# A sparse-attention block in which VectorE's step is turned round and the pass that pushes scores down goes to GpSimd

## What is computed

```python
x = x + layernorm(attn(layernorm(x)))
x = x + layernorm(ffn(layernorm(x)))

# attn
k = concat([mem_k, x @ Wk]); v = concat([mem_v, x @ Wv])
dots = einsum('bhid,bhjd->bhij', q, k) * 64 ** -0.5
dots = einsum('bhij,hk->bkij', dots, pre_proj)
dots = where(jj - 16 > ii, -max, dots)              # causal, memory keys are seen by all
vk = top_k(dots, 64)[0][..., -1:]                   # the 64th largest of each row
dots = where(dots < vk, -max, dots)
attn = einsum('bhij,hk->bkij', softmax(dots), post_proj)
out = (attn @ v) @ Wo + bo

# ffn
down((silu(gate(x)) * up(x)))                       # weights int32 / 127
```

## Time and profile before

| | |
|---|---|
| median of 3 runs | 3637.55 us (3636.05 to 3637.64) |
| the profiled execution, time | 3636.07 us |
| the profiled execution, span from first to last instruction | 3634.3 us |
| busy VectorE / ScalarE / TensorE / GpSimd | 3292.4 / 3199.3 / 2795.9 / 1551.4 us |
| mean granted TensorE clock | 0.884 |

### The profile page before, as it was taken

One profiled execution on the slowest core, in us unless ns is written; L12 is line 12 of the kernel. 1 busy time (PEld: TensorE's weight loads), 2 busy tenths in 40 slices (PEclk: granted clock), 3 DMA queues, 4 the chain that ended last, 5 costly groups with the idle time before them and its releaser, 6 DMA issues. The chain is left out here.

```text
span 3634.3 us, 67348 instructions
## 1 busy us (share of the span) xinstructions
PE 2795.9 (77%) x13751; PEld 1808.7 (50%) x13751; DVE 3292.4 (91%) x12492; ACT 3199.3 (88%) x9018; POOL 1551.4 (43%) x2663
## 2 busy tenths in 40 slices
PE   7777778777777878778778867877777788877765
PEld 3455455545545545555455545544555455545544
DVE  4699999999999999999999999999999999999994
ACT  1799999999979999999999979998999999999973
POOL 3233444444434444444444444443444444444433
PEclk9888999988888899888998888899889998899886
DMA  1000000000000000000000000000000000000000
GB/s 41 7 2 2 5 8 5 8 2 5 8 4 8 5 8 2 5 8 5 8 5 7 2 4 8 5 8 2 5 8 5 8 5 8 2 5 8 2 7 4
DMA packets 31375, 22.37 MB, mean 6 GB/s; under 512 B 3201, under 2 KB 30338, under 8 KB 30722
## 3 DMA queue, kind: packets, MB, share of 16 engines
q1 hardware_dynamic: 30722, 16.03, 1.6%
HBM read 11.83 MB, written 4.19 MB: 4 GB/s over the span
## 5 line engine op out<-in xcount | busy, mean ns | idle before, releaser
L871 ACT ACTIVATE signs<-scores,state 128x528 int8<-128x528 f32 (+3 forms) x3072 | 1764.3, 574 | 181.8 <-DVE state L1149 103.4
L713 PE MATMUL s_bank<-xn,gT 128*128 128x512 f32 (+3 forms) x2048 | 900.6, 568 | 1.7 <-issue 0.7
L1269 POOL TENSOR_SCALAR probs<-probs,rinv 128x528 f32<-128x528 f32 (+3 forms) x1024 | 547.1, 553 | 507.3 <-DVE rinv L1053 507.3
L737 PE MATMUL t_bank<-ident,probs 128*128 128x128 f32 x2560 | 482.7, 313 | 299.1 <-POOL probs L1269 289.7
L724 PEld LDWEIGHTS y_bank<-u_all,probsT 128*128 128x128 f32 x5120 | 619.9, 194 | 133.4 <-issue 124.2
L724 PE MATMUL y_bank<-u_all,probsT 128*128 128x128 f32 x5120 | 625.2, 278 | 7.1 <-ACT probsT L882 7.1
L1260 POOL TENSOR_TENSOR offset<-consts,found 128x36 f32<-128x36 f32 x256 | 161.7, 632 | 1047.5 <-DVE work L1014 1047.5
L871 ACT ACTIVATION_READ_ACCUMULATOR signs<-scores,state 128x1 f32 x3072 | 575.7, 187 | 0.0
L737 PEld LDWEIGHTS t_bank<-ident,probs 128*128 128x128 f32 x2560 | 299.7, 153 | 506.8 <-issue 398.6
L1048 DVE SCALAR_TENSOR_TENSOR probs<-scores,kth,expo 128x528 f32<-128x528 f32 (+3 forms) x1024 | 522.8, 565 | 24.8 <-issue 19.1
L892 ACT ACTIVATE expo<-scores,negmax 128x528 f32<-128x528 f32 (+3 forms) x1024 | 535.0, 575 | 0.0
(11 more groups left out here) (148 smaller groups left out, 3384.9 us busy)
## 6 DMA issues: line engine op xcount, KB each, us to landing
xwork<-in_L_attn_x_dram SPq DMA_DIRECT2D x17, 256.0 KB, 2.8
xres<-in_L_attn_x_dram SPq DMA_DIRECT2D x16, 256.0 KB, 2.9
out_dram<-ybuf SPq DMA_DIRECT2D x16, 256.0 KB, 2.4
u_all<-in_L_attn_Wq_dram SPq DMA_DIRECT2D x1, 512.0 KB, 3.7
u_all<-in_L_attn_Wk_dram SPq DMA_DIRECT2D x1, 512.0 KB, 4.5
u_all<-in_L_attn_Wv_dram SPq DMA_DIRECT2D x1, 512.0 KB, 5.3
u_all<-in_L_attn_Wo_dram SPq DMA_DIRECT2D x1, 512.0 KB
expo<-in_L_ffn_w_gate_dram SPq DMA_DIRECT2D x1, 192.0 KB, 4.7
```

The source lines that it names most:

```text
L713: nc.tensor.matmul(score_part(t, 0, KEYS[t]), lhsT=gT[s % 2][:, t * P:(t + 1) * P], rhs=xn[par][:, 0:KEYS[t]], start=True, stop=False, ski ...
L737: mm = nc.tensor.transpose(t_bank[q % 2][:, at:at + P], probs[:, h % 2, KEY_AT[t] + j * P:KEY_AT[t] + (j + 1) * P], ident[:, :])
L871: nc.scalar.activation(signs[:, k, 0:ROW[t]], row(scores, ring(head_of(s, k + 1), RING), t), ACT.Sign, bias=guesses(s % STATES, k, GUESSES ...
L1269: nc.gpsimd.tensor_scalar(prb, prb, rinv[:, slot_p, t:t + 1], 1.0, ALU.mult, ALU.mult).then_inc(scaled, 1)
```

## The change

- The push-down leaves VectorE. GpSimd does it in four instructions, one a tile, `work = scores - work`, once the count of that tile is there; a new semaphore `hidden` counts them. It subtracts 1 and not FMAX, so all scores are kept scaled by 2^-60 (the factor goes into `a_all`, `amem`, the guess table, `minus_unit` and the exponential's `scale`), and the causal mask is -2^40.
- VectorE's step is turned round. It begins with the four MAX8, pick and kth of head g-5 (the head that was counted one step earlier), with the flag loaded between the second and the third MAX8; then two counts of head g-4, the masked products and `rinv`, the other two counts, the eviction, `spread` and `missed`, the LayerNorm statistics, memory maxima or feed-forward product of that step, and the guess chain at the end.
- GpSimd's step: `negmax`, seed, memory scores, scaling, then the four push-downs, `offset`, `pmem`.
- TensorE makes the third part of the transposes ahead of the flag's matmul, ScalarE takes it ahead of the flag.
- Of the extras of a batch, U 8 to U 15 and DOWN move to other places of the list, the feed-forward product on VectorE from s = 10 to 12 to s = 11 to 13, the last LayerNorm from s = 14 to s = 15.

```diff
-MASKED = -2.0 ** 100
+UNIT = 2.0 ** -60
+MASKED = -2.0 ** 40
...
-                        turn(head_of(s, LAG_P), g - LAG_P, 0)
-                        turn(head_of(s, LAG_P), g - LAG_P, 1)
+                        for q in range(3):
+                            turn(head_of(s, LAG_P), g - LAG_P, q)
-                    if lagged(kind, s, LAG_P):
-                        turn(head_of(s, LAG_P), g - LAG_P, 2)
...
+                                                 scale=1.0 / UNIT
...
+                    if applies:
+                        dve.wait_ge(hidden, 4 * gp + 4)
+                        alone(dve)
+                        for p, t in enumerate(ORDER):
+                            if p == 2:
+                                dve.wait_ge(misc_free, flag_index(kind, b, s) + 1)
+                                alone(dve)
+                                rows_missed = dve.value_load(flags[0:1, T:T + 1].bitcast(I32), min_val=0,
+                                                             max_val=2 ** 31 - 1)
+                            v.max(candidates(past)[:, t, 1:9], work[:, AT[t]:AT[t] + ROW[t]]).then_inc(select_step, 1)
+                        dve.wait_ge(offset_ready, gp + 1)
+                        dve.wait_ge(select_step, T + 1)
+                        v.scalar_tensor_tensor(out=offset[:, :, 0:9], in0=offset[:, :, 0:9], scalar=0.0,
+                                               in1=candidates(past), op0=ALU.is_equal,
+                                               op1=ALU.mult).then_inc(select_step, 1)
+                        dve.wait_ge(select_step, T + 2)
+                        dve.sem_clear(select_step)
+                        v.tensor_reduce(kth[:, bass.ds(slot_p, 1), :].squeeze(1), offset[:, :, :], AX_X,
+                                        ALU.add).then_inc(kth_ready, 1)
                     if selects:
                         guessed = guesses(now, GUESSES, 1)
                         dve.wait_ge(guess_ready, g - 1)
                         dve.wait_ge(mem_placed, gk + 1)
                         dve.wait_ge(masked, 4 * gk + 4)
                         alone(dve)
-                        count_found(ORDER[0])
-                        count_found(ORDER[1])
+                        for t in ORDER[:2]:
+                            count_found(t)
                     if applies:
-                        dve.wait_ge(misc_free, flag_index(kind, b, s) + 1)
-                        alone(dve)
-                        rows_missed = dve.value_load(flags[0:1, T:T + 1].bitcast(I32), min_val=0, max_val=2 ** 31 - 1)
-                    if selects:
-                        count_found(ORDER[2])
-                        count_found(ORDER[3])
...
+                    if selects:
+                        for t in ORDER[2:]:
+                            count_found(t)
...
+                    if selects:
+                        dve.wait_ge(found_ready, 4 * gk + 4)
+                        v.scalar_tensor_tensor(out=spread[:, :], in0=found[:, :], scalar=-2.0 * AIM, in1=found[:, :],
+                                               op0=ALU.add, op1=ALU.mult).then_inc(select_step, 1)
+                        dve.wait_ge(select_step, 1)
+                        v.scalar_tensor_tensor(out=missed[:, 0:T], in0=spread[:, :], scalar=WINDOW ** 2 + 0.5 - AIM ** 2,
+                                               in1=active, op0=ALU.is_gt, op1=ALU.mult,
+                                               accum_out=missed[:, T:T + 1]).then_inc(bad_ready, 1)
...
+                    if 11 <= s < 11 + HC and kind != "first":
+                        c = s - 11
+                        dve.wait_ge(silu_pool, HC * (b - 1) + c + 1)
+                        v.scalar_tensor_tensor(out=f_up[:, c, :], in0=f_tanh[:, c, :], scalar=1.0,
+                                               in1=f_up[:, c, :], op0=ALU.add, op1=ALU.mult).then_inc(silu_ready, 1)
...
-                        v.scalar_tensor_tensor(out=work[:, :], in0=work[:, :], scalar=-FMAX,
-                                               in1=scores[:, bass.ds(slot_k, 1), :].squeeze(1),
-                                               op0=ALU.mult, op1=ALU.add).then_inc(select_step, 1)
...
-                    def top_scan():
-                        if selects:
-                            dve.wait_ge(select_step, 2)
-                            for t in ORDER:
-                                v.max(candidates(now)[:, t, 1:9], work[:, AT[t]:AT[t] + ROW[t]]).then_inc(select_step, 1)
...
-                    if lagged(kind, s, LAG_K):
-                        at_least(pool, kth_ready, g - LAG_K)
-                        pool.wait_ge(found_ready, 4 * (g - LAG_K) + 4)
...
+                    if lagged(kind, s, LAG_K):
+                        gk, slot_k = g - LAG_K, ring(head_of(s, LAG_K), RING)
+                        for p, t in enumerate(ORDER):
+                            pool.wait_ge(found_ready, 4 * gk + p + 1)
+                            alone(pool)
+                            wrk = work[:, AT[t]:AT[t] + ROW[t]]
+                            nc.gpsimd.tensor_tensor(wrk, row(scores, slot_k, t), wrk, ALU.subtract).then_inc(hidden, 1)
+                        at_least(pool, kth_ready, gk)
+                        alone(pool)
+                        nc.gpsimd.tensor_tensor(offset[:, :, 0:9], ranks, found[:, :].unsqueeze(2).to_broadcast([P, T, 9]),
+                                                ALU.add).then_inc(offset_ready, 1)
+                    if lagged(kind, s, LAG_P):
...
```

More of the change, by code:

```diff
@@ L84 @@
           11: [("GATE", 2), ("UP", 2)],
[L85 to L88, removed]
+          12: [("U", 10), ("U", 11)],
+          13: [("U", 12), ("U", 13)],
+          14: [("DOWN", 0), ("DOWN", 1)],
+          15: [("U", 14), ("U", 15)]}
 AIM = TOPK - 4
@@ L418, in build @@
         found_ready = sem("found_ready")
+        hidden = sem("hidden")
         offset_ready = sem("offset_ready")
@@ L913, in step @@
                     exponentials(3)
+                    take_turned(2)
                     if flagged(kind, s):
@@ L1063, in step @@
                                             accum_out=rowmax[:, bass.ds(slot, 1), t]).then_inc(masked, 1)
+                    if selects:
[6 more added lines that the diff above has]
+                                               accum_out=missed[:, T:T + 1]).then_inc(bad_ready, 1)
+                    if s == 0 and kind in ("first", "mid"):
+                        dve.wait_ge(x_in, 16 * (b + 2))
+                        norm_stats(kind, b, "x", xwork)
+                    if s == 8 and kind in ("first", "mid"):
+                        memory_maxima(kind, b, 1 - par)
                     if s == 6 and kind != "first":
@@ L1071, in step @@
                         norm_stats(kind, b, "X1", xres)
-                    if s == 14 and kind != "first":
+                    if 11 <= s < 11 + HC and kind != "first":
[3 more added lines that the diff above has]
+                                               in1=f_up[:, c, :], op0=ALU.add, op1=ALU.mult).then_inc(silu_ready, 1)
+                    if s == 15 and kind != "first":
@@ L1286, in step @@
                                               head_mem(smem[par], s)).then_inc(mem_placed, 1)
+                    gp, slot_p = g - LAG_P, head_of(s, LAG_P) % 2
+                    if lagged(kind, s, LAG_P):
+                        pool.wait_ge(rinv_ready, gp + 1)
+                        at_least(pool, probs_ready, 4 * gp + 4)
+                        alone(pool)
+                        for t in SCORE_ORDER:
+                            prb = probs[:, slot_p, AT[t]:AT[t] + ROW[t]]
+                            nc.gpsimd.tensor_scalar(prb, prb, rinv[:, slot_p, t:t + 1], 1.0, ALU.mult,
+                                                    ALU.mult).then_inc(scaled, 1)
+                    if lagged(kind, s, LAG_K):
[6 more added lines that the diff above has]
+                        at_least(pool, kth_ready, gk)
+                        alone(pool)
+                        nc.gpsimd.tensor_tensor(offset[:, :, 0:9], ranks, found[:, :].unsqueeze(2).to_broadcast([P, T, 9]),
+                                                ALU.add).then_inc(offset_ready, 1)
+                    if lagged(kind, s, LAG_P):
+                        if s == LAG_P and kind != "first":
+                            pool.wait_ge(misc_full, misc_index(kind, b, ("PM", 1)) + 1)
+                        pool.wait_ge(scaled, 4 * gp + 4)
+                        alone(pool)
+                        nc.gpsimd.tensor_copy(head_mem(pmem, head_of(s, LAG_P)), mem_parts(probs[:, slot_p, :])).then_inc(pmem_ready, 1)
                     extras(kind, b, s)
```

86 lines of the change are left out of this document (17 added, 69 removed).

## The result

| | before | after |
|---|---|---|
| median, us | 3637.6 (3636.05 to 3639.61, 4 runs) | 3796.25 (3793.69 to 3801.88, 4 runs) |
| ratio, 95% interval | | 1.0438 (1.042 to 1.0456) |
| span of the profiled execution, us | 3634.3 | 3800.0 |

The change makes the kernel 4.4% slower. The forecast was 2.4% slower (3724 us). The direction and the mechanism held; the size was off by 72 us. The time lies at the very end of the range of 3550 to 3800, and 6 us above the narrower 3660 to 3790 that the forecast had for itself.

A forecast was written before the change was run, and what follows sets the result against it. VectorE (201.3) and ScalarE (199.1 of 213.3 us a batch) bound it nearly level; 2.3 us of waiting replace 1.8 removed a plain step. 5.85 us times 14.5 batches is 85, plus 6, minus 3: 3636 + 88 = 3724 us, range 3550 to 3800.

The forecast's parts named there:

- L1124 and L1128 pass, L1131 loses to the fourth: VectorE's guess chain after L1123: two links get in at a pass boundary, the next stands until GpSimd's fourth pass ends, 11.8.
- the tail: End of the last batch before the change, where the guess chain meets back-to-back GpSimd passes and VectorE gets in at boundaries.
- the link that I had at 1.12 us from the end: L1139 in VectorE's guess chain: from it to the next MAX8 1.12 us, undisturbed after the fourth pass.
- Steps with extras: Steps with LayerNorm statistics 13.95 us each, memory maxima 13.85, s = 10 14.1, s = 11 and 12 14.6, s = 13 13.7.
- the sum: All steps of a batch added up: 219.15 us against 213.3, so 5.85 us a batch more.
- The upper end of the range: 3800 us, for GpSimd passes of 4.0 us in all: 0.4 to 0.5 us a step, 88 + 75 above.
- The reordering … I price at nothing: Turned step order, flag load between MAX8s, scaled constants and moved extras: the same instructions on the same engines, no cost.
- `missed` slips in: Rival, 0.18: `missed` gets in with `spread` at a pass boundary, plain steps 12.85, about 212 us a batch, 3616 us.
- The removed instruction was not the limit: Rival, 0.09: ScalarE is at its end in plain steps and the gain elsewhere is eaten, no change, 3637 us.
- ScalarE becomes the bound: Rival, 0.15 with waiting halved (3458 to 3560): ScalarE's stream limits at about 201.6 us a batch, 3458 us.
- GpSimd keeps the memory through its four passes: Rival, 0.10 with slower passes: `spread` stands until 11.8, plain step 14.0, batch near 235, about 3965 us.

The follow-up runs named there:

- e1: The changed kernel with its turned order kept but the push-down back on VectorE as one instruction between `spread` and `missed`: 3564.38 us, ratio to before 0.9794.
- e2: The changed kernel with GpSimd's four passes reading and writing `work` alone (times -1, scores left out, so results differ from the reference): 3497.66 us.
- e3: The changed kernel with GpSimd's four passes only writing `work` (memset, no read, push-down left out, so results differ from the reference): 3464.89 us.
- e10: The changed kernel with GpSimd's four push-downs merged into one instruction of 1344 columns behind the scaling: 3866.19 us.
- e9: The changed kernel with one wait, for all four counts, ahead of GpSimd's four push-downs and none between them: 3793.42 us.
- e7: e5 with the flag's load and two of the counts ahead of the products, and the one-input extras ahead of MAX8: 3852.62 us, ratio 1.0592.
- e5: The changed kernel with VectorE's order changed so that scaling and push-down on GpSimd meet only single-input counts, eviction and MAX8: 3767.79 us, ratio 1.0355.
- e11: e1 with only the flag's register load moved, from between the second and third MAX8 to right ahead of the branch: 3677.42 us.

## Why the prediction was right, and where its size was off

**Direction and mechanism: right.** The four passes take 1.30, 1.03, 0.77 and 0.57 us in the mean (forecast 1.30, 1.03, 0.75, 0.48; the fourth takes 0.49 in all but three steps of a batch), stand right behind the scaling, and lie over `spread`, `missed` and the guess chain. `spread` and `missed` were to end at 9.65 and 10.65 us of the step; they end at 9.56 and 10.55. `pmem` fell from 1.45 to 0.24 us, and MAX8 waits for `hidden` for 4 us in the whole run. ScalarE's idle time ahead of its counts grew by 0.86 us a step, where half a microsecond was forecast. e1, e2, e3 and e10 show the cause by taking it away, weakening it and making it longer.

**The step that failed is "L1124 and L1128 pass, L1131 loses to the fourth".** (In the changed kernel L1123, L1124, L1128 and L1131 are L1128, L1129, L1133 and L1136.) I took from the tail that a second instruction can follow on one that got in. In the changed kernel one passes at each boundary and no more. L1129 loses to the fourth pass too, 0.54 us, and the chain goes on from L1133 at 1715.74 instead of from the link that I had at 1.12 us from the end: 1.67 us are left. Against that the passes end at 11.70 of the step and not at 11.8. The plain step is 13.30 to 13.33 and not 13.05, 1.9 us a batch in seven steps. e9 rules out that GpSimd's waits make the difference to the tail; why L1124 and L1128 both got in behind L1123 there is open. The tail's passes have one input, but with one-input passes in e2 `missed` and L1129 stand as well (`missed` 461 and L1129 318 ns).

**Steps with extras: too low by about as much again.** From `rinv` to `rinv`, the 14 middle batches grew by 135.4 us, 9.67 each, where the sum had 5.85. Of these 3.8 us, 1.9 are those of the plain steps, and 0.25, 0.8 and 0.2 come from s = 10, 11 and 12 (14.35, 15.4 and 14.8 us in the mean against 14.1, 14.6 and 14.6). The rest, some 0.7, is spread over the others: s = 13 has 0.3 of it, and s = 1, 2 and 4, which the sum took for plain, are at 13.6, 13.8 and 13.5 in the mean. In s = 11 to 13 the sum had the feed-forward product at its 0.61 us and named it a two-input instruction, but gave neither it nor GpSimd a wait for it: the product takes 1.33 us there instead of 0.69, and GpSimd's fourth pass, which meets it, 0.9 instead of 0.49. 14 x 3.8 = 53 us of the missing 72 are in the middle batches. The first batch grew by 14.8 and not 6 us, and the last one by 12.2: I had spared both without ground, as every step in them has the same collision.

**The upper end of the range was reached in another way than the one that it was made for.** It stood for passes of 4.0 us in all, and they took 3.5. Its sum doesn't come out either: 0.4 to 0.5 us a step over some 240 steps is 96 to 120 us, not 75. That the time lies inside by 4 us is luck in part.

**"The reordering … I price at nothing" was wrong too, and hid in the sum.** e1 shows that the turned order, with the moved extras, gains 73 us: without the searches its batches take about 208.4 us against 213.2, its plain steps 12.0 to 12.9, 12.5 in the mean as before. The gain comes in steps with extras, where the guess chain's links that stood for GpSimd's work in the old order (by the names of before product L1128 363 ns, L1149 287, L1123 238 in the mean) are at 183, 197 and 165 in e1. One of these collisions has only moved: in s = 10 to 12 it is `missed` that now stands for `f_up * f_gate` (338 ns in the mean, 186 before). Which part of the change gives the gain was not tried apart. So the move of the pass costs 6.5% of e1, and the reordering hides a third of it.

**The rivals.** "`missed` slips in" falls with 955 ns. "The removed instruction was not the limit" (3637 us) falls with 159 us of change. "ScalarE becomes the bound" falls for the change, but e2 and e3 end at 3498 and 3465 us, inside its 3458 to 3560: e3's time is about what the move would give if GpSimd's passes did not read from SBUF. "GpSimd keeps the memory through its four passes" falls at the boundaries and comes true when the four are one (e10), at 3866 and not 3965 us.

## What to carry to other kernels

Before moving work from VectorE to GpSimd, write down which VectorE instructions will run beside it and count their SBUF inputs: with two, the GpSimd time that lies beside them is added to VectorE's again, whatever the size of the VectorE instruction. Here the pass took 1.55 us on VectorE, and on GpSimd it cost the kernel 0.9 us a step more. A chain of small dependent instructions is the worst neighbour, since only one of them gets in where a GpSimd instruction ends. And when a step is laid out anew, see what covers a register load ahead of a branch, and add up the loop through the other engine, not only one engine's work (e7).

## What was not expected of the hardware

- One small VectorE instruction, and not two, gets in between back-to-back GpSimd passes (L1128 0.58, L1129 0.37 us in the mean against 0.16 and 0.17), with or without semaphore waits between them.
- GpSimd passes that only write `work` (542 ns for 528 columns) leave VectorE's two-input instructions at 159 and 168 ns.
- A flag's register load and the branch on it cost VectorE 1.55 us of a plain step with nothing queued ahead (e5), 0.61 us behind 1.3 us of counts (e11), and nothing to be seen (10 us of issue time in the whole run) with two MAX8, the pick and two counts between them.
- One GpSimd instruction that reads SBUF does not hold VectorE: the power operation of LayerNorm on 4 elements (`rstd`, L1185, 1.04 us). In the changed kernel a two-input VectorE instruction started under it, with over 0.1 us of it left past the normal end, 177 times and took at most 0.06 us over its normal time; under the four passes that was so 577 times, each at least 0.24 us over. So the theory of the experiments has a gap here; whether the few elements or the kind of operation make it was not tried. GpSimd's line, then VectorE's beside it:

```profile
1520.24 1.04 POOL L1185 TENSOR_TENSOR rstd<-vareps,minus_half 128x4 f32<-128x4 f32 x1
```

```profile
1520.25 0.22 DVE L1144 TENSOR_TENSOR state<-state,between 128x24 f32<-128x24 f32 x1
1520.50 0.18 DVE L1146 TENSOR_TENSOR apart<-state 128x24 f32<-128x24 f32 x1
```

- GpSimd waits for VectorE in the same way: in e1 the feed-forward product `f_up * f_gate`, started 0.01 us after VectorE's whole push-down of 1.55 us, took 2.67 us, where it takes 1.28 in the kernel before.
